# A fused attention and local-transformer kernel: shifted input rows by two transposes and ten small DMAs a tile, and a new order of the work on every engine

## The reference, cut to what matters

```python
x = attn_layer(shift_tokens(x), Wqkv[i], q_scale[i], k_scale[i], Wo[i]) + x
x = ffn_layer(shift_tokens(x), ln_g[i], ln_b[i], W1[i], b1[i], W2[i], b2[i]) + x
```

## Time and profile before

| what | us |
| --- | --- |
| median of 3 runs | 2095.5 (2095.35 to 2100.75) |
| the profiled execution's own time | 2100.06 |
| its span, first to last instruction | 2098.2 |
| mean granted TensorE clock | 0.979 of full |
| TensorE matmuls (PE) busy | 1924.6 (92%) |
| VectorE, ScalarE, GpSimd busy | 1560.9, 1290.3, 1324.6 |

### The profile page before, as it was taken

One profiled execution on the slowest core, in us unless ns is written; L12 is line 12 of the kernel. 1 busy time (PEld: TensorE's weight loads), 2 busy tenths in 40 slices (PEclk: granted clock), 3 DMA queues, 4 the chain that ended last, 5 costly groups with the idle time before them and its releaser, 6 DMA issues. The chain is left out here.

```text
span 2098.2 us, 65778 instructions
## 1 busy us (share of the span) xinstructions
PE 1924.6 (92%) x27244; PEld 1523.1 (73%) x27244; DVE 1560.9 (74%) x2684; ACT 1290.3 (61%) x2082; POOL 1324.6 (63%) x1145
## 2 busy tenths in 40 slices
PE   6888886699999999999999999999999999999996
PEld 4665665577777777777777777777777877787774
DVE  4766865777887778877777877788776878787773
ACT  5666765356566656665656666657665666566654
POOL 2332343677786667776667866588666777676760
PEclk9999998899999999999999999999998999999999
DMA  3000001000000010000010000100000100000000
GB/s 99 2 0 0 0 1 57 15 3 2 2 2 2 2 55 2 2 3 2 2 55 2 2 2 2 55 3 2 2 2 6 52 2 2 2 3 6 2 7 16
DMA packets 12434, 25.12 MB, mean 12 GB/s; under 512 B 1856, under 2 KB 9728, under 8 KB 10496
## 3 DMA queue, kind: packets, MB, share of 16 engines
q1 hardware_dynamic: 12160, 21.16, 2.9%
HBM read 20.11 MB, written 1.05 MB: 10 GB/s over the span
## 5 line engine op out<-in xcount | busy, mean ns | idle before, releaser
L1061 PE MATMUL banks<-arena 128*128 128x128 f32 (+4 forms) x6052 | 672.8, 311 | 60.0 <-ACT arena L689 16.8
L1061 PEld LDWEIGHTS banks<-arena 128*128 128x128 f32 (+3 forms) x6052 | 558.5, 176 | 169.8 <-issue 70.6
L902 DVE TENSOR_TENSOR arena<-banks,tabs 128x1024 f32<-128x1024 f32 x192 | 235.2, 1225 | 133.6 <-ACT arena L646 125.0
L449 POOL TENSOR_TENSOR arena<-arena 128x1024 f32<-128x1024 f32 x96 | 230.6, 2402 | 66.0 <-DVE arena L907 65.8
L479 POOL TENSOR_TENSOR small<-small 128x33 f32<-128x33 f32 x100 | 24.6, 246 | 350.2 <-ACT small L736 350.2
L675 ACT ACTIVATE arena<-banks 128x1024 f32<-128x1024 f32 x96 | 98.7, 1028 | 238.2 <-PE banks L1218 238.2
L444 POOL TENSOR_TENSOR prob<-prob,small 128x1024 f32<-128x1024 f32 x96 | 182.7, 1903 | 82.9 <-DVE small L942 82.9
L907 DVE TENSOR_TENSOR arena<-banks,tabs 128x1024 f32<-128x1024 f32 x192 | 233.3, 1215 | 0.2 <-issue 0.2
L454 POOL TENSOR_TENSOR arena<-arena 128x1024 f32<-128x1024 f32 x96 | 228.7, 2382 | 4.0 <-DVE arena L907 4.0
L1218 PEld LDWEIGHTS banks<-cst,arena 128*128 128x128 f32 x1536 | 182.1, 142 | 28.9 <-issue 2.9
L1218 PE MATMUL banks<-cst,arena 128*128 128x128 f32 x1536 | 201.3, 275 | 1.0 <-ACT arena L675 1.0
(11 more groups left out here) (132 smaller groups left out, 3993.1 us busy)
## 6 DMA issues: line engine op xcount, KB each, us to landing
qkraw<-in_wqk_dram SPq DMA_DIRECT2D x6, 1024.0 KB, 5.5
arena<-in_wvo_dram SPq DMA_DIRECT2D x6, 1024.0 KB, 7.1
W<-in_w_dram SPq DMA_DIRECT2D x6, 341.0 KB, 8.6
W<-in_w_dram SPq DMA_DIRECT2D x6, 192.0 KB, 2.3
res<-in_x_dram SPq DMA_DIRECT2D x4, 256.0 KB, 4.2
tabc<-in_tab_dram SPq DMA_DIRECT2D x1, 1024.0 KB, 6.2
out_dram<-res SPq DMA_DIRECT2D x4, 256.0 KB, 2.3
sca_s<-in_sca_dram SPq DMA_DIRECT2D x6, 128.0 KB, 3.4
```

The source lines that it names most:

```text
L449: pool.tensor_tensor(kc, kc, ks, ALU.add).then_inc(s["k_add"], 1)
L902: dve.tensor_tensor(heads(c), heads(two(0)), table(k % NT, kind), ALU.mult).then_inc(s[done], 1)
L1061: return pe.matmul(o, l, r, start=start, stop=stop)
```

## The change

The input rows. `windows` and `copy_windows` go. In their place `input_rows` makes two transposes a tile (`X`, unshifted features and shifted features, into banks 2 and 3), `copy_input_rows` copies the 128x128 rows into `xr`, and SyncE cuts them into the windows with ten DMAs from SBUF to SBUF a tile: two of 32 rows and three of 64 rows for each of two row halves. `xw` and `xr` are double-buffered. `weigh_lower` waits on the DMAs' semaphore, SyncE on the copy and on the `weigh` of two tiles ago.

The weights. `W2` gets two buffers. SyncE issues each load of the next layer behind a tile of its own (tiles 2, 5, 7, 10, 12 and 13). The steps that prepare weights become calls of their own, with places of their own in the loops.

The order. The calls of all four loops are in another order, some with the step counted differently. There are 107 steps in place of 108. `LAST_GELU` is 1 in place of 2.

```diff
-STEPS = DEPTH * TILES + 12
+STEPS = DEPTH * TILES + 11
-M_BANK, XW, DN_BANK = 7, 4, 7
-LAST_GELU = 2
+XD = 10 * 16
+XT_COL = 0
+M_BANK, XT_BANK, DN_BANK = 7, 2, 7
+LAST_GELU = 1
...
+            for k in range(LAST_TILE + 1):
+                l, n = divmod(k, TILES)
+                sp.wait_ge(s["xT_cp"], k + 1)
+                if k > 1:
+                    sp.wait_ge(s["z_mm"], 2 * k - 2)
+                now, was = xr[:, k % 2, :], xr[:, (k + 1) % 2, :]
+                for o in range(2):
+                    c0 = 64 * o
+                    sp.dma_start(xw[c0:c0 + WIN, k % 2, 0, :], was[96:P, :]).then_inc(xd_in, 16)
+                    sp.dma_start(xw[c0 + WIN:c0 + 64, k % 2, 0, :], now[0:WIN, :]).then_inc(xd_in, 16)
+                    for w in range(1, NW):
+                        sp.dma_start(xw[c0:c0 + 64, k % 2, w, :], now[WIN * (w - 1):WIN * (w + 1), :]).then_inc(xd_in, 16)
+                if n == 2 and l + 1 < DEPTH:
...
+            def copy_input_rows(k):
+                if is_tile(k):
+                    act.wait_ge(s["xT_mm"], k + 1)
+                    if k > 0:
+                        act.wait_ge(xd_in, XD * k)
...
+            def input_rows(k):
+                if is_tile(k):
+                    b, i = tile_at(k)
+                    after(pe, "x_new", k // 4 - NC + 1)
+                    claim(XT_BANK, XT_BANK + 1)
+                    for z in range(2):
+                        r = slice(64 * z, 64 * z + 64)
+                        c0 = XO + P * i - z
+                        ins = pe.transpose(bk(XT_BANK + z)[:, XT_COL:XT_COL + 64], X[r, b, c0:c0 + P], ident[r, 64 * z:64 * z + 64])
...
```

More of the change, by code:

```diff
@@ L329, in _ @@
             load_w2(0)
+            load_w2(1)
             load_par(0)
@@ L512, in _ @@
             for G in range(STEPS):
[L513 to L523, removed]
+                scale_queries(G - 1)
+                scale_probs(G - 2)
+                next_key_weights(G)
+                rotate_keys(G)
+                shifted_lower(chunk_at(G, 14))
+                lookback(G)
+                refine(G)
+                scale_keys(G)
+                next_query_weights(G)
+                lower_columns(G - 5)
+                rotate_queries(G)
                 next_table(G - 1)
@@ L769, in _ @@
             for G in range(STEPS):
[L770 to L774, removed]
+                copy_queries_T(G - 2)
                 gelu(chunk_at(G, 10), 2)
+                copy_probs(G - 3)
+                roots(G - 1)
                 copy_columns(G - 6)
[L777 to L781, removed]
+                copy_input_rows(G - 2)
                 copy_rows(G - 4)
@@ L785, in _ @@
                 copy_lower(G - 3)
+                next_folded_lower(G - 4)
+                next_w1_upper(chunk_at(G, 12))
                 exponentials(G - 2)
+                gelu(chunk_at(G, 9), 0)
+                shifted_upper(chunk_at(G, 14))
+                next_key_upper(G)
+                next_folded_upper(G - 4)
                 copy_upper(G - 3)
+                gelu(chunk_at(G, 9), 1)
+                square_queries(G)
+                next_query_upper(G)
         @block.vector
@@ L1019, in next_biases, with next_w1_lower @@
                     biases(c // NC + 1)
+            def next_w1_lower(c):
+                if c is not None and c % NC == NC - 1 and c < DEPTH * NC - 1:
+                    w1_lower(c // NC + 1)
             def residual(c):
@@ L1432, in _ @@
             for G in range(STEPS):
+                up_value(chunk_at(G, 11), 0)
+                down(chunk_at(G, 13))
+                weigh_upper(G - 4)
+                next_products_upper(G - 5)
+                project_queries(G - 1)
+                transpose_queries(G - 2)
+                up_gate(chunk_at(G, 10), 2)
+                mask_scores(G - 2)
+                fold_lower(G - 4)
+                transpose_probs(G - 3)
+                scores(G - 2)
+                ln_columns(G - 6)
+                fold_upper(G - 4)
+                input_rows(G - 2)
+                project_keys(G)
                 ln_rows(G - 4)
-                project_keys(G)
                 transpose_keys(G - 1)
+                next_shifts(chunk_at(G, 13))
                 weigh_lower(G - 3)
+                up_value(chunk_at(G, 11), 2)
+                next_products_lower(G - 4)
+                up_gate(chunk_at(G, 9), 0)
+                up_gate(chunk_at(G, 9), 1)
                 up_value(chunk_at(G, 10), 1)
-                up_value(chunk_at(G, 10), 0)
-                up_gate(chunk_at(G, 9), 0)
-                next_shifts(chunk_at(G, 12))
-                up_value(chunk_at(G, 11), 2)
-                up_gate(chunk_at(G, 9), 1)
-                down(chunk_at(G, 12))
-                weigh_upper(G - 3)
-                project_queries(G)
-                transpose_queries(G - 1)
-                windows(G - 2)
-                up_gate(chunk_at(G, 9), 2)
-                fold_lower(G - 3)
-                ln_columns(G - 5)
-                mask_scores(G - 1)
-                fold_upper(G - 3)
-                scores(G - 1)
-                transpose_probs(G - 2)
-                last_rows(chunk_at(G, 14))
+                last_rows(chunk_at(G, 13))
 _OUT = ("out_0_dram", (B, T, D))
```

129 lines of the change are left out of this document (68 added, 61 removed).

## The result

| | before | after |
| --- | --- | --- |
| median, us (4 runs each) | 2098.12 | 2149.11 (2144.38 to 2157.68) |
| profiled execution, us | 2100.06 | 2144.38 |
| span, us | 2098.2 | 2142.6 |
| granted TensorE clock | 0.979 | 0.983 |

The changed kernel is slower, by the ratio 1.0244 [1.02, 1.0287] (in brackets the 95% interval); the prediction was 2187, range 2125 to 2260. The profiled executions are 44.3 us apart.

The account below looks back on a forecast made before the run. TensorE bounded the kernel before; two table loads in each step's roots were to lengthen the steps. 2100.06 + 104 (loads) + 15 (clock) - 28 (seams) = 2191, or 2187 in the runs' terms; range 2125 to 2260.

Parts of the forecast that it names:

- Two loads in every step's roots: ScalarE's roots: `Ln` and `Exp` each get an unnamed table load, 2.57 us a step; chance 0.84.
- The rival by which one set serves both functions: ScalarE's roots: one load of the joint set serves until the next gelu, time 2067; chance 0.08.
- The loop: Path from transposed keys through roots and `scale_keys` back: 14.15 us a plain step, 16.7 with two loads; group 71.6.
- the term +104: Steps from the first gelu 2 on: +4.8 us a chunk over 21.75 chunks, +104 us.
- The low clock, +15: TensorE standing still behind loads lowers its granted clock: +15 us for the run, bounds 0 and 148.
- Seams, -28: Seams between layers: spread weight preparation saves 5.6 of 15.5 us a layer, -28 us; bounds 0 and -78.
- Input rows, swallowed while the loads bound: TensorE's input rows: 0.41 us a tile less, -39 us if TensorE stays the bound, swallowed in the +104.
- That the DMAs hide: Ten input-row DMAs a tile take 7.7 us overlapped, wanted some 18 us later: cost nothing; late-DMA rival's chance 0.03.
- GpSimd's wait for `Exp` "at least as long": Sign of being right: GpSimd's wait for ScalarE's `Exp`, 350.2 us before, doesn't get shorter.
- with the loads hidden: Rival: TensorE stays the bound and loads are hidden, -39 - 28, time 2028; chance 0.02.

Follow-up runs that it names:

- experiment 6: Changed kernel with the joint table set named ahead of each `Ln`, `LAST_GELU` still 1: 2085.82 us, ratio 0.9931 to the kernel before.
- experiment 1: Changed kernel with `LAST_GELU` = 2, so the joint table set is named behind the last gelu again: 2061.15 us, ratio 0.9805 to the kernel before.
- experiment 4: Changed kernel with `LAST_GELU` = 2 and input rows by the 16 small matmuls of before, without the DMAs: 2073.08 us, ratio 0.9853 to the kernel before.
- (3): Changed kernel with the old order of the four loops, old places of weight preparation and `LAST_GELU` = 2: 2094.3 us, ratio 0.9979 to the kernel before.
- (8): Changed kernel with `LAST_GELU` = 2, `rotate_keys` ahead of `scale_probs` on GpSimd, `normalise_rows` behind `sine_keys` on VectorE: 2026.17 us, ratio 0.9635.
- experiment 9: Changed kernel, `LAST_GELU` left at 1, with `rotate_keys` ahead of `scale_probs` and `normalise_rows` behind `sine_keys`: 2174.14 us, ratio 1.0362 to the kernel before.
- the two moves: `rotate_keys` ahead of `scale_probs` on GpSimd, `normalise_rows` behind `sine_keys` on VectorE; on top of experiment 1: 2026.17 us.
- experiment 2: Kernel before the change with `LAST_GELU` = 1 and nothing else: 2263.8 us, ratio 1.0766 to the kernel before.

## Why the prediction was right

The mechanism was right: table loads that no line names in every step's roots, on the path, and a longer step by what they and the chunk's work add. The size was not: +91 us were forecast in the profiled executions' terms and 44 measured. The time lies in the range because the range was wide.

**Two loads in every step's roots: right.** 91 and 91 of them, 256 in all against "some 250", and each of 1283 ns. The activation behind a load starts 1.29 us after the load does (1419.73 and 1421.02), as in the earlier trace rows.
The Trainium skill (ScalarE: Activation LUTs, What ACT_TABLE_LOAD costs) adds a drain of some 1380 ns to each; by that a step would have been 2.8 us longer than it is. No row here shows it.
The rival by which one set serves both functions (Table sets: the hidden batching unit, on the same page) held only where the code names the joint set: experiment 6 has one load a step, the changed kernel two.

**The loop: right for this group, and it was the core of the forecast.** Plain step 16.7 against 16.50, with `down` 18.3 against 18.07, gates 19.7 against 19.27, two value products 16.9 against 17.02; group 71.6 against 70.86. What a sum of durations and starts on one path gave was within 0.5 us in every step. In one place it was right by another cause: in the step with two value products TensorE's stall was for VectorE's sine product (1.20 us), not for the scaled keys. Measured from the groups, the term +104 was (70.86 - 66.82) x 21.75 = +88; experiment 1 against the changed kernel gives 88 too, by taking the loads out, but not the same 88: its groups are only 2.6 us shorter (68.24), since the collision bounds there, and more comes from its seams (a layer is 13.9 us shorter, 10.5 of it in the groups) and a shorter end.

**The low clock, +15: wrong.** TensorE's stalls of 0.8 to 1.6 us didn't bring it down: the granted clock is 1.00 in the group, and the time at half speed from 350 us on fell from 70.9 to 62.9 us. By the prediction's own price, half of such a stretch, that is -4.

**Seams, -28: right in kind, too small.** Its 5.6 us a layer are also mis-added: a stall of 2.0 and 3.6 us at half speed counted in full, where the clock's term prices such a stretch at half; that would be 3.8 a layer and -19. A layer of 289.4 us less 4 x 70.86 = 283.4 leaves 6.0 against 15.5; over five layers -47. +88 and -47 make +41 of the 44.3 measured. The split depends on the group taken as the measure: the layer of before has some three steps of 20 to 23 us in other places, the changed one a single one of 20.4 to 22.3. What is sure is their sum, a layer of 289.4 us against 282.7. With my +104, +15 and -28 it was +91: the three terms erred in the same direction, 16, 15 and 19 us, together 50 us, and nothing made up for it. In the profiled executions' terms 2191 lies 47 over 2144.38; in the medians' 2187 lies 38 over 2149.11.

**Input rows, swallowed while the loads bound: right.** They give 12 us where VectorE's collision bounds (experiment 4), some 4 in the old order (3), and with TensorE as bound (8) the group is 0.9 to 2.0 us shorter than before. That the DMAs hide: right, landed after 7.8 us where 14.9 or more are there.

**What I looked for and wasn't there.** GpSimd's wait for `Exp` "at least as long": it got shorter, as the idleness moved ahead of `scale_probs`. And I had checked GpSimd and VectorE by their busy time per group against its length, where both fitted. The premise was that an operation keeps its duration when it is moved; 109 us of VectorE say otherwise. In the changed kernel this lengthening lies beside the path in the plain step: the seeds are through at 1419.44, the load ahead of `Ln` at 1421.01. It doesn't in all steps: the sine product stands behind these operations, and TensorE waits 50.4 us for it in the whole span. What that cost the changed kernel was not isolated, as experiment 9's moves made it slower. For the rivals it was no detail: with the loads hidden I had worked out 2028, and experiment 1, without the extra loads, stops at 2061.15. It takes the two moves to reach 2026.17, and that this is so near to 2028 is partly luck, since it is another order than the one forecast.

## What to carry to other kernels

A load of ScalarE's tables that no line of the code shows is worth a search before any other estimate: go through the engine's order once, with the set after each activation written beside it, and follow what stands behind the switch. Price it on the loop of one step, by starts and durations of one path, not by busy shares: the same 206 loads cost 88 us in one order and 159 to 166 in another, and a single load in a plain step's roots cost nothing. And when an order is changed, compare the mean duration of every operation before and after, on the engines that were not meant to change.

## What the runs showed of the hardware

- A `tensor_scalar` on VectorE with 33 f32 elements a partition (L992), 0.18 us alone, took up to 1.93 us in experiment 1 and 2.06 in the changed kernel when it began under a GpSimd operation, and ended with it within 0.1 us. Small `tensor_tensor`s with both inputs in SBUF did so too (L997, 0.19 us alone, up to 1.78). A product from PSUM (L939) kept its 1.21 us under the same kind of operation (at 1326.05 in experiment 1, under L507), in all 192 executions.
The Trainium skill (GPSIMD Engine Reference, 1. Specifications) lists GpSimd's SBUF interfaces as shared with VectorE, with contention for vector instructions in a 2-port mode or with two SBUF inputs; VectorE: DVE Perf Modes (Mode 2×_2P) has f32 `tensor_scalar` in such a mode. The rows agree as to which operations suffer.
- An SBUF-to-SBUF DMA of 16 or 32 KB: 0.59 us to issue in the median of 960 (0.47 to 1.81), 1.8 and 1.9 us from issue to landing in the median (1.7 to 4.0).
- With no set named behind the last gelu, `Ln` and `Exp` got a load each in every one of 91 steps: 182 loads (changed kernel; experiment 2 has the same 182).
